# More products of ones on TensorE in a four-layer convolution and attention kernel: in the first pair, ahead of each even part, and at the norm

## What is computed

```python
x = L0(x)   # channel attention per image (energy = q q^T, softmax), gate se: se*x + (1-se)*out
x = L1(x)   # 1x1 reduce to 64, depthwise 3x3, BN, relu; fft2; attention over Fourier features
            # per head; a gated Fourier filter; ifft2; 1x1 post over both, + x
x = L2(x)   # group norm; 8-head attention over the 256 pixels of an image; projection; + x
x = L3(x)   # q, k, v = conv3x3(x); per pixel, attention between the 16 images;
            # norm of each image over all its channels and pixels; relu; conv3x3; + x
```

## Time and profile before

| what | value |
|---|---|
| median of 3 runs | 523.4 us (523.14 to 523.52) |
| the profiled execution: its own time | 525.22 us |
| its span on the core | 523.4 us |
| mean granted TensorE clock | 0.966 |
| busy: PE, DVE, ACT, POOL | 476.1, 353.3, 263.9, 136.6 us |
| products of ones (PE L1209) | 224 |

### The profile page before, as it was taken

How to read it: one execution, slowest core, us unless ns; L and a number is a source line. 1 busy time by engine, 2 the same in 40 slices (tenths; PEclk the granted TensorE clock), 3 DMA queues, 4 the chain that set the end, 5 groups by cost and what they waited for, 6 DMA issues and landing times.

```text
span 523.4 us, 10554 instructions
## 1 busy us (share of the span) xinstructions
PE 476.1 (91%) x3746; PEld 377.3 (72%) x3746; DVE 353.3 (68%) x895; ACT 263.9 (50%) x654; POOL 136.6 (26%) x161
## 2 busy tenths in 40 slices
PE   8698899989999999999999999989988998785895
PEld 7575766668687767767776877667676788785885
DVE  1628737895778678686967777784467345675995
ACT  4235466664646454555546464443534514984540
POOL 5320663261013102210410221030110012504662
PEclk9999869999999999999999999998997999997999
DMA  5000111000000000000000000000000000004111
GB/s 219 21 20 3 45 46 43 24 21 23 0 21 22 1 0 20 20 0 0 20 20 0 20 0 0 2 22 0 1 7 15 1 22 1 1 0 162 43 59 61
DMA packets 9488, 13.18 MB, mean 25 GB/s; under 512 B 496, under 2 KB 8816, under 8 KB 9328
## 3 DMA queue, kind: packets, MB, share of 16 engines
q1 hardware_dynamic: 9456, 12.76, 7.3%
HBM read 8.56 MB, written 4.19 MB: 24 GB/s over the span
## 4 chain that ended last, share of the span: by engine, by line
PE 60%; DVE 23%; issue 8%; ACT 7%; DVEq 1%; POOL 0%; ACTq 0%
PE bank L1202 7%; PE bank L1403 5%; PE bank L1204 5%; PE bank L1203 5%; PE bank L1321 5%; PE bank L1377 4%; PE bank L1209 3%; DVE nmax L995 3%; PE bank L1353 2%; PE bank L1375 2%; PE bank L1390 2%; PE bank L1431 2%; ACT x L801 2%; PE bank L1226 2%; DVE even L895 2%
## 5 line engine op out<-in xcount | busy, mean ns | idle before, releaser
L1202 PE MATMUL bank<-win,w_hi 128*128 128x256 f32 x384 | 121.4, 316 | 12.7 <-DVE win L1148 5.9
L1203 PE MATMUL bank<-win,w_hi 128*128 128x256 f32 x384 | 108.8, 283 | 0.0
L1204 PE MATMUL bank<-win,w_lo 128*128 128x256 f32 x384 | 108.8, 283 | 0.0
L743 ACT ACTIVATE prob<-bank 128x512 f32<-128x512 f32 x128 | 69.6, 597 | 76.1 <-PE bank L1375 75.3
L995 DVE TENSOR_REDUCE nmax<-bank 128x2 f32<-128x512 f32 x128 | 85.4, 685 | 27.9 <-PE bank L1353 27.3
L1202 PEld LDWEIGHTS bank<-win,w_hi 128*128 128x128 f32 x384 | 73.3, 191 | 24.0 <-issue 11.2
L1203 PEld LDWEIGHTS bank<-win,w_hi 128*128 128x128 f32 x384 | 73.5, 191 | 0.5
L1204 PEld LDWEIGHTS bank<-win,w_lo 128*128 128x128 f32 x384 | 73.2, 191 | 0.0
L520 POOL TENSOR_TENSOR first<-first 128x256 f32<-128x256 f32 x24 | 17.8, 740 | 167.6 <-ACT first L632 167.6
L1377 PE MATMUL bank<-qk 32*128 32x256 f32 x256 | 41.6, 341 | 3.0 <-ACT prob L743 2.6
L1209 PE MATMUL bank<-ones_r 128*128 128x256 f32 x224 | 39.8, 318 | 1.1 <-DVE ones_r L849 1.1
(11 more groups left out here) (237 smaller groups left out, 933.9 us busy)
## 6 DMA issues: line engine op xcount, KB each, us to landing
w_stage<-convs SPq DMA_DIRECT2D x4, 576.0 KB, 3.8
x_in<-x SPq DMA_DIRECT2D x8, 256.0 KB, 2.7
out<-x_pair SPq DMA_DIRECT2D x8, 256.0 KB, 2.2
q<-out SPq DMA_DIRECT2D x1, 2048.0 KB, 8.3
out<-v SPq DMA_DIRECT2D x8, 256.0 KB, 2.1
cst<-small SPq DMA_DIRECT2D x1, 1708.0 KB, 8.3
cst<-small SPq DMA_DIRECT2D x1, 253.5 KB, 2.9
```

The source lines that it names most:

```text
L743: act.activation(prob[:, x // 4 % 2, x % 4, :, :], bank[ST_BANK[x % 2]][:, :], ACT.Exp, scale=L2_SCALE).then_inc(st_exp, 1)
L1202: mm(dst, hi, x_hi, start=(row == 0), stop=False)
L1203: mm(dst, hi, x_lo, start=False, stop=False)
L1204: return mm(dst, lo, x_hi, start=False, stop=(row == KH - 1))
```

## The change

It does three things. `BUSY_PAIR_0` gets three products of ones in each of slots 5 to 15 of pair 0 (33 products). Where work of the pair before is left (`left`: pairs 2 to 6), TensorE waits before `even` until that pair's convolutions are joined, and then issues five products into the convolutions' bank (25 products). After the last sum of the norm it issues 34 products.

```diff
-BUSY_AHEAD, BUSY_PAIR_0, BUSY_PAIR_1 = 14, {1: 6, 2: 6, 3: 6, 4: 6, 16: 6, 17: 6, 18: 6, 19: 6}, {s: 3 for s in range(13)}
+BUSY_AHEAD, BUSY_EVEN, BUSY_PAIR_1 = 14, 5, {s: 3 for s in range(13)}
+BUSY_PAIR_0 = {1: 6, 2: 6, 3: 6, 4: 6, **{s: 3 for s in range(5, 16)}, 16: 6, 17: 6, 18: 6, 19: 6}
...
+BUSY_NORM = 34
...
                     for what, i in parts(PE_SLOTS, s, early, late):
+                        if what == "even" and left:
+                            pe.wait_ge(joined, 3 * cj)
+                            keep_busy(BUSY_EVEN, CONV)
                         stage(what, i)
...
             pe.wait_ge(w_split, 4)
+            keep_busy(BUSY_NORM)
```

## The result

The changed kernel takes 520.9 us (median of 22 runs, 519.09 to 524.13) against 524.19 us (22 runs, 522.26 to 525.51) of the kernel before beside it: a ratio of 0.9938, 95% interval 0.9924 to 0.9952, 3.3 us less. The forecast was 4.0 us less, 0.9924. Executions of one kernel lie up to 5 us apart (519.09 to 524.13), and the experiments show a large part of the reason.

A forecast was written before the change was run, and what follows sets the result against it. TensorE, busy for 91% of the span, and four stretches at 1.2 GHz were taken as the bound. -1.2 (pair 0) + 0.3 (even) - 3.1 (pair 6) + 0 (norm) = -4.0, from 523.4 to 519.4 us; range 517.2 to 524.4.

The forecast's parts named there:

- Pair 0: Slots 5 to 15 of pair 0: 33 products keep the clock up, -1.2 us, bounds -0.4 and -2.0.
- the walk through the slots: Pair 0's step times: slot 8 0.5 later, slot 12 0.4 earlier, then 1.4, `y1` 1.0 to 1.7, exponential 1.1 to 1.55.
- Ahead of even: Before `even` in five pairs: 25 products fill the waits and overrun slightly, +0.3 us, bounds 0 and 3.5.
- Pair 6: From `even` on in pair 6: the low stretch goes, -3.1 us, bounds 0 and -3.4.
- The norm: After the norm's last sum: 34 products fit the gap and hold the clock, worth 0, bounds -1.7 and +0.9.
- the upper bound of the norm: At the norm: +0.9 us if 34 products at 0.25 ran at the low clock, less VectorE's slack of 1.91.
- rival 1: Pair 0 keeps its low clock and its products cost about 5 us, 4 net: 524.6 us, slower than before; 13%.
- The second: Pair 0 is won but the clock falls elsewhere, in pair 6, a middle pair or pair 1: 522.4 us; 15%.
- The third: Everywhere: the products don't hold the clock at all, 528.7 us at most, 527.8 with some absorbed; 7%.
- The fourth: More is won: pair 7's low stretch falls differently or is shorter, or the norm gives 1.7: 517.7 us; 10%.

The follow-up runs named there:

- the 32-row kernels: The changed kernel with products of ones over 32 rows, not 128: only the 92 new ones (523.55 us, 0.9987), or all 316 (545.27 us, 1.0442).
- experiment 1: Only the 33 products in slots 5 to 15 of pair 0, added to the kernel before: 521.83 us, ratio 0.9966.
- Experiment 8: The changed kernel with fifteen products ahead of each even part instead of five: 527.22 us, ratio 1.0066 to the kernel before.
- experiment 2: Only the 25 products ahead of the even parts, added to the kernel before: 523.74 us, ratio 0.9981.
- experiment 4: The changed kernel without the norm's 34 products: 520.86 us, ratio 0.9945 to the kernel before.
- second session: The changed kernel measured again, unchanged: 521.64 us, ratio 0.9948 to the kernel before.
- experiment 3: Only the 34 products at the norm, added to the kernel before: 523.99 us, ratio 0.9990.
- experiment 12: The changed kernel with all 316 products of ones over 32 rows and not 128: 545.27 us, ratio 1.0442 to the kernel before.
- look 2: A second more profile of the kernel before, unchanged: span 522.2 us, pair 0 46.30 us.

## Why the prediction was right, and where its sizes were off

**Pair 0 (-1.2 forecast).** This execution had reached pair 0 1.72 us later than that of before, behind two low stretches of its start-up, and won 1.45 of it back by slot 5, since the one of before had a low stretch at 51 us. What remained is the 0.27 at the last step before slot 5. Less that, the walk through the slots held closely: L1377 of slot 8 0.24 later and not 0.5; slot 12 0.41 earlier, as said, though TensorE waited 0.38 for POOL's b_signed before `dot1` (L1281), a gap that pair 1 has not, so here two errors cancel; `filt` 1.40 earlier, as said; `y1` 1.32, in the range of 1.0 to 1.7; the exponential behind the weight split 1.32, in that of 1.1 to 1.55. Pair 0 itself went from 45.70 to 42.91, 2.8 less: 1.3 by this and 1.45 by the low stretch at 51 us, in slots where the change puts nothing. Over the profiles with the 33 products it took 43.4 on average (six: 42.89 to 44.19), without them 44.7 (six: 42.75 to 46.30; the 32-row kernels are left out), 1.3 less. The timed runs of experiment 1 say 1.8. What the walk did not foresee is that pair 0 of the kernel before is at times without this low stretch, and then there is nothing to win: 42.80 us in the profile of the even products alone, against 42.89 to 43.13 in the four profiles with the 33 products and no low stretch.

**Ahead of even (+0.3).** Pairs 2 to 5 kept their 47.4 us; the four together became 0.06 us longer, as the gap before L1283 took the products in, where 0.3 was forecast for five places. Experiment 8 shows the price where the gap is full.

**Pair 6 (-3.1): the term that was mis-sized.** In the two profiled executions it is right to 0.05 us: 48.15 to 45.10. But I took a low stretch of one execution for one of every execution. Without the five products (and without 32-row ones) it was in one of six profiles, with them in none of five; so few profiles do not show that the five keep it away. As means, 45.60 against 45.08 are 0.5 us; the timed runs of experiment 2 say 1.0, from 2.4 less to 0.4 more. So the term is about 0.5 to 1.0, perhaps nothing, and not 3.1.

**The norm (0).** Right: 51.6 to 51.8 us in every profile with full-array products, with the 34 and without, with 3 to 10 us of low clock around it or none. That they keep the clock up there was right in part. From 474 us on it is 1.00, as forecast, but in the changed kernel a low stretch of 3.4 us began as they began, behind the gaps between the last sums, and what it stretched was products of ones. Over the profiles with full-array products, the stretch at the norm is 3.4 us (three) or absent (two) with the 34, and 6.8 to 10.2 us (seven) without.

**The sum.** By the ratios the three parts alone give 1.8 + 1.0 + 0.5 = 3.3 us, and together they gave 3.3. That they agree so well is partly luck: each part's interval is about 1.3 us wide to either side, and by the medians the parts give 2.1, 0.2 and -0.1. The time at 1.2 GHz per execution, worked out from the granted clock of every timed run as in experiment 4, adds up more firmly. The kernel before has 30.8 us of it; the parts take away 5.8 (pair 0), 2.5 (even) and 6.6 (norm), 14.9 together (each with a standard error of 1.2 to 1.6), and the whole change 14.7 in its second session (31.9 to 17.2). Most of what the norm's products take away is worth nothing, as experiments 3 and 4 show. The 92 products over 32 rows take away 3.5.

So the forecast of 4.0 came near by luck as well: pair 6's term was given 3.1 and brought 0.5 to 1.0, while pair 0 brought 1.3 to 1.8 where 1.2 was given. The profiles account for 1.3 + 0.5 of the 3.3, and where the rest is won stays open.

Two slips in the prediction's arithmetic have no part in this: the upper bound of the norm is 480.5 - 477.9 - 1.9 = 0.7 and not 0.9, and rival 1 breaks even where 2.2 of its 5 us are returned, which leaves a cost of 2.8.

**The rivals.** The first (pair 0 keeps the low clock) came in none of the six profiles with the 33 full-array products: slots 5 to 15 had no low stretch there, where three of the six without them had one. The second (a fall elsewhere, because later work comes at other times) was in neither profile of the changed kernel, but falls of this kind are real: pair 1 fell with the even products alone and with 32-row ones, for 3.4 us and 0.6 us of time. The third is out with the norm and with experiment 12. The fourth came in another form: pair 7 could be won, but with products of its own.

## What to carry to other kernels

Where TensorE's clock falls in a profile of a kernel with gaps and narrow products, that place is a candidate and not a fact: take three profiles before pricing it, and price it by how many of them show it. The place to fill first is the one that is low in all of them, here pair 7, 15 products for 2.2 us, which the change had left out. A filler product should use all 128 rows: with 32 it took as long and did not hold the clock (fewer columns were not tried). It should stand where the engine waits anyway, and costs 0.10 to 0.14 us as soon as it does not. And a low clock is worth removing only where other engines wait for TensorE: at the norm it cost nothing.

## What the runs showed of the hardware that was not expected

- The same kernel, unchanged, has its low stretches in different places from one execution to the next: 65-75, 81-88 and 64-78 us in pair 0. What one costs differs: 3.4 us of it cost nothing in pair 0 of experiment 3 (42.75 us, against 42.80 with none) and 0.6 in pair 1 of experiment 2 (47.9 against 47.3); 6.8 us cost 3.1 in pair 6; 13.7 us cost 3.5 in pair 0 of look 2.
- TensorE was busy for 21 us without a gap and stayed at half the clock (experiment 12), with products of ones over 32 rows between the kernel's own.
- The clock column shows 1.00 where there is no record yet. The duration of a known product is the check: 0.12 us from start to start for 256 columns at the full clock, 0.21 to 0.25 at half.
